# A last phase with another order of its evictions, 16 record scatters in an earlier block, and a weight split ahead of the first expert tile

## What is computed

```
x = x + GIN(layernorm(x))              # edge sum, then 256-512-1024-512-256
                                       # with batch norm and elu
x = x + MoE(layernorm(x))              # 8 experts, 2 for each node,
                                       # w2(silu(w1 x) * (w3 x)), hidden 682
x = x + GAT(layernorm(x))              # 4 heads of 64, softmax over edges:
    out = elu(sum(w * x[dst]) / rowsum + b)
n = layernorm(x)                       # the last phase
logit = n . wr + br; keep the 1561 nodes with the largest logits
y = (gelu(n @ w1 + b1) @ w2 + b2) * logit    # hidden 1024, kept nodes only
x = x + n + y
```

## Time and profile before

| | us |
|---|---|
| median of 3 runs (lowest, highest) | 2238.18 (2237.57, 2238.66) |
| the profiled execution's own time | 2233.31 |
| its span | 2231.6 |
| busy: PE, DVE, POOL, ACT | 1826.7, 1377.4, 1365.6, 658.0 |
| mean granted clock of PE | 0.812 |

### The profile page before, as it was taken

One profiled execution on the slowest core, in us unless ns is written; L12 is line 12 of the kernel. 1 busy time (PEld: TensorE's weight loads), 2 busy tenths in 40 slices (PEclk: granted clock), 3 DMA queues, 4 the chain that ended last, 5 costly groups with the idle time before them and its releaser, 6 DMA issues. The chain is left out here.

```text
span 2231.6 us, 36642 instructions
## 1 busy us (share of the span) xinstructions
PE 1826.7 (82%) x9636; PEld 1301.8 (58%) x9637; DVE 1377.4 (62%) x3195; ACT 658.0 (29%) x1301; POOL 1365.6 (61%) x1358
## 2 busy tenths in 40 slices
PE   2888889998899798754899999748878888884888
PEld 2766667776344344652666666546655556663666
DVE  7676654444665686886633333247777777776666
ACT  4000000000455665632633333232111111112764
POOL 3777777774377776456666666527777777773000
PEclk8555555555899799855999999967999998986899
DMA  8333333332000301090222222251111111122002
GB/s 243 101 105 104 103 104 106 104 105 73 1 1 1 59 1 56 27 343 20 35 39 39 38 38 39 28 131 27 29 29 28 29 29 28 29 28 7 1 1 59
DMA packets 95358, 132.05 MB, mean 59 GB/s; under 512 B 34959, under 2 KB 66334, under 8 KB 95293
## 3 DMA queue, kind: packets, MB, share of 16 engines
q0 software_dynamic: 57312, 87.64, 18.0%
q1 hardware_dynamic: 37981, 43.65, 6.7%
HBM read 109.24 MB, written 21.96 MB: 59 GB/s over the span
## 5 line engine op out<-in xcount | busy, mean ns | idle before, releaser
L597 POOL DMA_INDIRECT rec_d<-rec,posd x392 | 414.1, 1056 | 168.1 <-issue 125.6
L1640 POOL DMA_INDIRECT g<-tab_d,recs x416 | 395.6, 951 | 163.6 <-issue 126.5
L497 PE MATMUL psA<-oh,G 128*128 128x128 f32 x1568 | 440.0, 445 | 65.5 <-DMA G<-xn_d,gat_i 33.4
L312 POOL DMA_INDIRECT G<-xn_d,gat_i x392 | 376.8, 961 | 146.1 <-issue 136.8
L497 PEld LDWEIGHTS psA<-oh,G 128*128 128x128 f32 x1568 | 348.8, 311 | 156.6 <-issue 98.1
L1789 PE MATMUL psS<-vv,oh 128*125 128x260 f32 x832 | 284.1, 486 | 97.3 <-DVE acc L1721 94.4
L841 PE MATMUL psZ<-z,W 128*128 (+1 forms) x1344 | 264.0, 359 | 26.0 <-DVE z L740 26.0
L1789 PEld LDWEIGHTS psS<-vv,oh 128*125 128x125 f32 x832 | 156.2, 220 | 196.0 <-DVE acc L1721 169.8
L447 DVE TENSOR_TENSOR accT<-accT,psA 128x256 f32 x392 | 165.0, 421 | 167.0 <-PE psA L497 141.0
L643 ACT ACTIVATE z<-psZ,vec 128x500 f32 (+2 forms) x112 | 70.8, 634 | 638.6 <-PE psZ L834 528.9
L841 PEld LDWEIGHTS psZ<-z,W 128*128 128x128 f16 x1344 | 124.5, 98 | 165.6 <-issue 38.4
(11 more groups left out here) (318 smaller groups left out, 2434.6 us busy)
## 6 DMA issues: line engine op xcount, KB each, us to landing
raw<-in_L_ffn_w SPq DMA_DIRECT2D x16, 682.0 KB, 11.6
g<-tab_d,recs POOLq DMA_INDIRECT x416, 2.5
G<-xn_d,gat_i POOLq DMA_INDIRECT x392, 2.7
rec_d<-rec,posd POOLq DMA_INDIRECT x392
raw<-in_L_ffn_w SPq DMA_DIRECT2D x16, 384.0 KB, 12.1
wst<-in_L_gnn_W SPq DMA_DIRECT2D x9, 512.0 KB, 6.9
x<-in_x SPq DMA_DIRECT2D x5, 560.0 KB
xn_d<-x SPq DMA_DIRECT2D x5, 560.0 KB
```

Of the source, the lines that this page charges most:

```text
L312: pool.indirect_dma_start(out=G[:, i, :], out_offset=None, in_=xn_d, in_offset=bass.IndirectOffsetOnAxis(ap=gat_i[:, t:t + 1], axis=0)).th ...
L497: last = nc.tensor.matmul(psA[i // 2][:, i % 2, h, :], G[:, i, 128 * h:128 * (h + 1)], oh[:, i, :], start=True, stop=True)
L597: pool.indirect_dma_start(out=rec_d.rearrange("p (t r) -> (p t) r", r=2), out_offset=bass.IndirectOffsetOnAxis(ap=posd[:, t:t + 1], axis=0 ...
L1640: pool.indirect_dma_start(out=g3[:, n % BODY, j, :], out_offset=None, in_=tab_d, in_offset=bass.IndirectOffsetOnAxis(ap=recs[:, t, 1:2], a ...
```

## The change

Three edits.

1. `EDGES_EARLY` 264 and `EDGES_ROUTER` 16: sixteen records move from the router stage to the layers' block.
2. The six pieces of expert 2 are split, on ACT and DVE, right after the placement is known and before the first `halves_x`, not between the evictions of tile 0.
3. The last phase. `fold` is cut in three: `unit` (the min/max, L2000), `fold` (the addition, L2001) and `stats6`. DVE sets `lower` and `low_x` between them; the second group's statistics come after the first two `low_x`. ACT takes the exponential before the next turns' `high_x`, and `norm(c + 1)` in the middle of chunk c (before: `norm(c + 2)` at its end); `twice(c)` comes before the third `high_x`. PE sums count 5 after product 7 of chunk 4 (before: after product 5).

```
-        EDGES_EARLY = 248
-        EDGES_ROUTER = 32
+        EDGES_EARLY = 264
+        EDGES_ROUTER = 16
...
                 act.wait_ge(s_where, 1)
+                for third in range(3):
+                    later_w(0, third)
                 halves_x(0, 0)
                 halves_x(1, 1)
                 silu(0, 0, True)
-                later_w(0, 0)
                 silu(0, 1, True)
-                later_w(0, 1)
-                later_w(0, 2)
...
+                for third in range(3):
+                    later_w(0, third)
                 halves_x(0, 0)
                 halves_x(1, 1)
                 hidden(0, 0, 0)
-                later_w(0, 0)
                 hidden(0, 0, 1)
-                later_w(0, 1)
-                later_w(0, 2)
...
                 norm(0)
-                for g in range(3):
+                for g in range(2):
                     high_x(g)
                 spread(1)
...
                         gelus(c, m, n)
                         n += 1
-                        if c == 0 and m == 3:
-                            norm(1)
+                        if c == 0 and m == 0:
+                            high_x(2)
+                        if c < 4 and m == 3:
+                            norm(c + 1)
+                    if c < 3:
+                        lifted(c + 2)
                     if c < 4:
                         high_x(3 * c + 3)
                         high_x(3 * c + 4)
                     if c < 3:
-                        lifted(c + 2)
-                        spread(c + 2)
+                        twice(c)
                     if c < 4:
                         high_x(3 * c + 5)
                     if c < 3:
-                        norm(c + 2)
-                    if c < 5:
+                        spread(c + 2)
+                    if c in (3, 4):
                         twice(c)
...
+                unit(0)
                 fold(0)
+                stats6(0)
                 scales6(0)
+                unit(1)
                 fold(1)
-                for g in range(3):
+                for g in range(2):
                     low_x(g)
+                stats6(1)
                 scales6(1)
...
+                        if c == 0 and m == 0:
+                            low_x(2)
...
+                    if c < 3:
+                        unit(c + 2)
+                        low_x(3 * c + 3)
+                        lower(b0)
+                        fold(c + 2)
+                        low_x(3 * c + 4)
+                        lower(b0 + 1)
+                        stats6(c + 2)
+                        lower(b0 + 2)
+                        low_x(3 * c + 5)
+                        scales6(c + 2)
+                        lower(b0 + 3)
+                        continue
+                    if c == 3:
                         low_x(3 * c + 3)
                         low_x(3 * c + 4)
-                    if c < 3:
-                        fold(c + 2)
...
-                        if c == 4 and m in (1, 5):
+                        if c == 4 and m in (1, 7):
                             total(4 + m // 4)
```

More of the change, by code:

```diff
@@ L1992, in lift, with unit @@
                     nc.vector.tensor_tensor(o_, o_, bgb[:, :].unsqueeze(1).to_broadcast([PB, 5 * NH, OD]), ALU.add).then_inc(s_og, 1)
-                def fold(c):
-                    cs = slice(5 * c, 5 * c + 5)
+                def unit(c):
                     e_ = eg[:, c % 4, :, :]
@@ L1999, in fold, with stats6 @@
                     dve.wait_ge(s_eg, c + 1)
-                    ch.step(nc.vector.scalar_tensor_tensor(e_, e_, 1.0, og[:, cs, :], ALU.min, ALU.max))
-                    ch.step(nc.vector.scalar_tensor_tensor(x2[:, cs, :], e_, -1.0, x2[:, cs, :], ALU.add, ALU.add))
+                    ch.step(nc.vector.scalar_tensor_tensor(e_, e_, 1.0, og[:, 5 * c:5 * c + 5, :], ALU.min, ALU.max))
+                def fold(c):
+                    cs = slice(5 * c, 5 * c + 5)
+                    ch.step(nc.vector.scalar_tensor_tensor(x2[:, cs, :], eg[:, c % 4, :, :], -1.0, x2[:, cs, :], ALU.add, ALU.add))
                     dve.sem_inc(s_fold, 1)
+                def stats6(c):
+                    cs = slice(5 * c, 5 * c + 5)
                     for b in range(5):
@@ L2157, in _ @@
                                 finish(14 + m // 2)
-                    if c < 4:
+                    if c < 3:
[12 more added lines that the diff above has]
+                    if c == 3:
                         low_x(3 * c + 3)
                         low_x(3 * c + 4)
-                    if c < 3:
-                        fold(c + 2)
                     for b in range(b0, b0 + nb):
                         lower(b)
-                        if c < 4 and b == b0 + 1:
+                        if c == 3 and b == b0 + 1:
                             low_x(3 * c + 5)
-                        if c < 3 and b == b0 + 1:
-                            scales6(c + 2)
                         if c == 3:
```

## The result

The changed kernel takes 2217.81 us (median of 4 runs, 2216.15 to 2219.09) beside 2238.27 us of the kernel before (4 runs, 2237.57 to 2238.66): ratio 0.9909, 95% interval 0.9891 to 0.9926. It is faster by 20.5 us. The profiled execution took 2217.62 us with a span of 2215.9, so it lies on its median, while that of before lay 5.0 us under its own; between the two profiles only 15.7 us are seen.

A forecast was written before the change was run, and what follows sets the result against it. PE's waits and fallen clock in the last phase and POOL's late first fetch in the router stage were taken as bounds; 8.0 + 15.9 - 0 = 23.9 us off the 2238.18 median gave 2214.3 us, range 2207 to 2222.5.

The forecast's parts named there:

- case A: Whole kernel: the prediction as worked, 23.9 us off, 2214.3 us; chance 0.52.
- B: Last phase: new waits in chunks 1 and 2 let the clock fall, 2.6 us a chunk, 2219.5 us; chance 0.20.
- C: Router stage: fetches wait for the split, first issued at 1036, 1.2 of 5.2 us left, 2218.3 us; chance 0.08.
- The counts 264 and 16: End of layers' block: sixteen more scatters end at 945.6, cost 0, bounds 0 and 1.4 us; first fetch 7.2 us earlier.
- The warning sign of the prediction's last paragraph: Block after the layers: the forecast is wrong if it begins more than 1 us later.
- Router stage and tiles: Router stage and experts' tiles: 5.2 us from earlier halves_x(0), 2.1 from tile 0's wait, 0.7 from the clock: 8.0 us.
- The last phase: Chunks 0 to 4: chunk 3 18.0 us earlier, less 2.2 and 1.4, plus 1.5: 15.9 us, bounds 10 and 21.
- The wait at the first count: After chunk 3: PE's wait of 2.52 us becomes 3.6; 1.4 us taken for the clock, between 0 and 2.6.
- The count moved in chunk 4: Chunk 4: the count moved behind product 7 takes away PE's wait of 1.50 us.
- D: Last phase: ACT becomes the bound, a chunk stays near 28 us, 2221.5 us; chance 0.12.
- E: Last phase: clock stays at 0.50 through chunks 1 to 3, 42.7 us slower, 2280.9 us; chance 0.03.
- F: Experts' tiles or after chunk 3: something unseen takes up the gains, change not measurable; chance 0.03.

The follow-up runs named there:

- run 5: The changed kernel, run again without an edit: 2211.55 us, ratio 0.9897 to the kernel before.
- run 2: The kernel before with the counts 264 and 16 alone: 2228.83 us, ratio 0.9969.
- run 7: The changed kernel with the first count product one down block later, behind the second of chunk 3: 2204.66 us, ratio 0.9864 to the kernel before.
- run 11: The changed kernel with the first count product one block later, counts 264 and 16, timed again in a series of counts: 2206.35 us, ratio 0.9879.
- run 4: The kernel before with the new order of the last phase alone: 2219.84 us, ratio 0.9935.
- run 6: The changed kernel with counts 256 and 24 instead of 264 and 16: 2210.56 us, ratio 0.9892 to the kernel before.
- run 1: The kernel before, unchanged, for a second profile: 2238.35 us.
- run 3: The kernel before with expert 2 split before the first tile, counts 248 and 32: 2232.49 us, ratio 0.9991.
- run 8: The kernel before with one more wait on DVE, so that it pauses between its one-hot rounds: 2231.61 us (one run).
- 272 and 8: The changed kernel with the first count product one block later and 272 early, 8 router scatters: 2218.97 us, ratio 0.9922 to the kernel before.

## Why the prediction was right, and where its steps failed

2217.8 us were measured for 2214.3 forecast, within the range; by its profile case A is what happened; the time alone would not tell it from B (2219.5) or C (2218.3). The sum of 23.9 us compares with 20.5 by medians here (16.6 to 24.4 by the ratio's interval) and 23.1 in run 5 (2234.68 - 2211.55).

**The counts 264 and 16: cost 0 forecast, bounds 0 and 1.4; 4.8 us measured in the profile.** This is the step that failed. It let the next block start as soon as the last scatter had ended, 945.6 against 946.3. In all six profiles with 264 or 272 early scatters the next block began only 3.57 to 4.22 us after the last of them had ended (3.57 in three). With the forecast end of 945.6 the shortest of these alone gives 949.2. Besides, the pace of the scatters was taken from their mean, and it differs between executions: the last of the 264 started between 941.06 and 948.10 in five profiles, the next block between 945.97 and 952.63, so from 0.6 us earlier than the 946.62 of before to 6.0 us later, 3.2 on average. POOL held the block in all five: DVE stood idle before it for 5.58, 0.83, 5.14, 1.65 and 3.15 us (the changed kernel, runs 2, 5, 7 and 11), where it was 0.32 in the kernel before, so the cost was between 0.5 and 5.3 us, about 3 on average. What makes the pace differ was not tried. The bound of 1.4 us was too tight. The warning sign of the prediction's last paragraph, a block that begins more than 1 us later, came true without taking the forecast with it. The other half held: counted from the block's start the first fetch was 6.8 us earlier, with the counts alone and in the whole change (7.2 forecast), and 16 scatters end before DVE's one-hot rounds.

**Router stage and tiles: 8.0 us forecast, 9.1 measured** against the block's start. `halves_x(0)` comes 5.5 us earlier there (5.2). The wait in tile 0 went from 3.60 to 1.50 (2.1 forecast, 2.1 measured), and the products behind it from 3.07 to 2.25 us, 0.8 instead of 0.7. The rest, 0.7 us, was not in the sum: behind the long wait the next tile's first products had been slow as well (tile 1's first 12 upward products took 2.69 us before and take 2.11 now). The fetches did not wait for the split (rival C): they were held for some 0.3 to 0.8 us each.

**The last phase: 15.9 us forecast, 14.3 in the two profiles, 14.5 by run 4's ratio.** Its steps:
- First product upward 3.7 us earlier forecast, 3.6 measured, against the phase's start.
- Chunk 1 9.0 us earlier forecast, 10.7 measured, since the wait at the end of chunk 0 is 1.12 us instead of 3.89 and no clock fell.
- Chunks of 24.5 us forecast, 24.6 and 25.0 measured. The new waits of 1.3 and 1.5 us are there in other places: in each of chunks 0 to 3 one of 0.35 or 0.36 and one of 0.68 before products whose halves come singly from DVE, and 1.12, 1.12 and 1.49 before the turns. Chunk 3 starts 19.1 us earlier (18.0).
- The wait at the first count, 3.6 us forecast, is 3.33. Behind it 1.4 us were taken for the clock between bounds 0 and 2.6; it cost 5.36 - 2.81 = 2.55, and 2.1 and 1.7 in the profiles of runs 4 and 6. In all, chunk 3 takes 30.2 us where it took 25.2 (5.0 more; 2.2 + 1.4 = 3.6 forecast), and chunk 4 starts 14.1 us earlier (14.4).
- The bound 0 for this term, and the argument against rival B, rested on one profile in which the clock stayed at 1.00 behind 2.52 us. That does not repeat. In the five profiles with the old last phase the wait is 2.52 or 2.53 us each time; the 24 products behind it take 2.81 us in two (before, run 2) and 4.14, 4.48 and 4.48 in three (runs 1, 3 and 8). Run 1, with a granted clock of 0.56 from 2170 to 2172:

```profile
2168.69 0.38 PE L2224 MATMUL psT<-cn,ones 125*125 125x1 f32 x2 [2.53 <-DVE xt L2027]
2168.93 4.14 PE L2215 MATMUL psD<-f,fh 128*125 128x256 f16 x24
```

- The count moved in chunk 4: 1.5 us were credited, and this term held. The kernel before waited twice, 1.50 us and 1.36 at the next count (row below); now only the second is left, with 1.25 us (2173.18). Chunk 4 takes 23.3 us instead of 25.2, so that chunk 5 starts 16.0 us earlier (15.9).

```profile
2190.57 0.39 PE L2224 MATMUL psT<-cn,ones 125*125 125x15 f32 x2 [1.36 <-DVE cn L2054]
```

- The final 120 products were not in the sum. They took 13.27 us in eleven of the fourteen profiles and 14.77 to 14.84 in three (the changed kernel, run 5, and 272 and 8), with a fallen clock. They are the 1.5 us that are missing at the end. The last of the three has no wait at the first count, so that wait is not the cause; it stays open.

The other rivals: the clock did not fall in chunks 1 and 2 (B; 5.45 us for 48 products, and no more than 5.46 in any of the nine profiles with the new order), ACT did not set the pace (D; chunks of 24.6, not 28), and E and F did not occur.

**The offset, and what was luck.** The sum was subtracted from the median, 4.9 us above the profiled execution. The changed kernel's profile lay on its own median. From profile to profile the span fell by 15.7 us, so the sum was 8.2 us too large there: 4.8 for the late block, 2.9 lost behind tile 1 in unchanged code, 1.6 in the last phase, less 1.1 gained in the router stage and tiles. That the forecast time is off by only 3.5 us is in part luck, since the offset stood against these. That the last phase's start moves by 4.6 us in unchanged code (run 1) shows how much such an offset is worth.

The Trainium skill, in "SBUF — State Buffer", "Who interferes with whom", infers that tensor_tensor leaves descriptor generation alone, because it takes only the read interface of the shared ports. The scatters here, which read their indices (`posd`) and their records from SBUF, were held beside tensor_tensor work: 3.94 us with a pause behind it (run 8), 19.42 us without. For such scatters the rows decide against the inference. Whether it is the generation that waits or a read from SBUF, which the same section lets contend with a two-input instruction, no run here tells.

## What to carry to other kernels

A queue of indirect DMAs that may run up to the end of a block should end some 4 us before it, plus the spread of its pace from run to run; put the rest where another wait covers it. A short product block in front of a wait of 3 us paid twice on PE, since without the wait the clock also stayed up: 3.3 us of waiting filled brought 5.7 in the profiles. Before an effect of under 5 us is read from two profiles, compare them from a common start inside the stage.

## What was not expected of the hardware

- A block that POOL holds ends 3.57 to 4.22 us after the end of its last scatter (next block's start 951.44, 945.97, 952.63, 951.07, 948.03 and 960.94). In the changed kernel's packed trace the last scatter has landed by 949.01, 2.4 us before the next block's first instruction; what fills the rest was not found.
- A scatter beside DVE's tensor_tensor rounds ends 0.83 us after DVE pauses, in all three cases above. In rounds 2 to 4 of run 8 one scatter of each (the first at 1011.63, 2.24 us) got through in the middle of a round, 0.83 us after the end of the round's second instruction (1013.04). Two-input scalar_tensor_tensor work of 5.3 us (the split) only lengthened each transfer by 0.3 to 0.8 us, and these too end 0.82 to 0.84 us after the end of one of its instructions (in run 3 at 1031.53, with the first piece through at 1030.70). So each of these transfers got through at the end of some instruction of DVE: in the kernel before only at the end of the fifteenth and last, elsewhere at the end of the one that ran when the transfer was issued, or of the next. What makes the difference is open and was not tried.
- The same wait of 3.33 us on PE cost between 1.7 and 2.55 us of slower products behind it in four profiles (4.48, 4.88, 5.36 and 5.36 us for a block that takes 2.81), and a wait of 2.52 or 2.53 us cost nothing in two profiles and 1.3 to 1.7 in three.
